# Attention heads of the fourth stage as one stream, their q and k stacked in pairs through DRAM

## The reference

```python
c_kv = h @ w_dkv.T
q = (h @ w_q.T).reshape(B, S, 16, 16)
k = (c_kv @ w_uk.T).reshape(B, S, 16, 16)
v = (c_kv @ w_uv.T).reshape(B, S, 16, 16)
scores = einsum('bqhd,bkhd->bhqk', q, k) * 0.25 + alibi_bias(S)   # -inf above the diagonal
attn = softmax(scores, axis=-1)
out = einsum('bhqk,bkhd->bqhd', attn, v).reshape(B, S, 256) @ w_o.T
x = x + out
```

## Time and profile before

| | us |
|---|---|
| median of 3 runs | 636.63 |
| lowest, highest | 632.98, 636.9 |
| the profiled execution | 632.82 |
| its span, from first to last instruction | 631.0 |
| PE busy, DVE, ACT, POOL | 580.0, 422.4, 250.6, 110.1 |
| mean granted TensorE clock | 0.888 of 2.4 GHz |

### The profile page before, as it was taken

One profiled execution on the slowest core, in us unless ns is written; L12 is line 12 of the kernel. 1 busy time (PEld: TensorE's weight loads), 2 busy tenths in 40 slices (PEclk: granted clock), 3 DMA queues, 4 the chain that ended last, 5 costly groups with the idle time before them and its releaser, 6 DMA issues.

```text
span 631.0 us, 9323 instructions
## 1 busy us (share of the span) xinstructions
PE 580.0 (92%) x3218; PEld 470.9 (75%) x3218; DVE 422.4 (67%) x1249; ACT 250.6 (40%) x525; POOL 110.1 (17%) x163
## 2 busy tenths in 40 slices
PE   1999999999789999999996798899998999989995
PEld 1888888888568888888885687656666666658885
DVE  3677985877863557748777999764542794315986
ACT  3557434642223433335336244323433363333341
POOL 1001000110110000001006428111211032213442
PEclk9999999999789999999999798955558995558999
DMA  5322202000000000000000300000000000000001
GB/s 174 105 96 76 84 28 57 18 2 0 1 1 1 1 1 2 1 0 2 2 0 2 134 21 1 1 1 0 2 2 1 0 2 1 2 0 2 1 34 34
DMA packets 7102, 14.01 MB, mean 22 GB/s; under 512 B 1296, under 2 KB 3600, under 8 KB 6928
## 3 DMA queue, kind: packets, MB, share of 16 engines
q1 hardware_dynamic: 6000, 12.91, 6.3%
q10 hardware_dynamic: 1056, 0.51, 0.3%
HBM read 12.37 MB, written 1.05 MB: 21 GB/s over the span
## 4 chain that ended last, share of the span: by engine, by line
PE 80%; DVE 11%; issue 4%; ACT 2%; POOL 1%; DMA 1%; ACTq 1%; DVEq 0%; POOLq 0%
PE ps L498 19%; PE ps L500 18%; PE ps L499 18%; PE ps L797 4%; PE ps L814 3%; DVE gel L1293 3%; PE ps L774 3%; PE ps L802 2%; PE ps L744 2%; PE ps L786 2%; PE ps L508 2%; PE ps L772 2%; PE ps L745 1%; DVE z L1215 1%; DVE gel L1291 1%
## 5 line engine op out<-in xcount | busy, mean ns | idle before, releaser
L498 PE MATMUL ps<-zh,w0u_h 128*128 128x512 f32 x256 | 102.4, 400 | 2.5 <-issue 2.5
L500 PE MATMUL ps<-zl,w0u_h 128*128 128x512 f32 x256 | 101.8, 397 | 0.0
L499 PE MATMUL ps<-zh,w0u_l 128*128 128x512 f32 x256 | 101.5, 396 | 0.0
L945 ACT ACTIVATE gel<-ps 128x512 f32<-128x512 f32 x64 | 38.2, 597 | 104.1 <-PE ps L500 103.9
L1311 DVE TENSOR_TENSOR act<-gel,ps 128x512 f32<-128x512 f32 x64 | 43.8, 684 | 52.7 <-ACT gel L945 52.7
L498 PE MATMUL ps<-w0d_h,ah 128*128 128x256 f32 x256 | 73.3, 286 | 1.3 <-DVE al L1318 1.0
L1571 DVE CUSTOM_DVE_ANT_0 ps<-ps,bias 128x128 f32<-128x128 f32 (+1 forms) x128 | 43.1, 381 | 44.2 <-PE ps L774 43.9
L499 PE MATMUL ps<-w0d_h,al 128*128 128x256 f32 x256 | 72.4, 283 | 0.0
L500 PE MATMUL ps<-w0d_l,ah 128*128 128x256 f32 x256 | 72.4, 283 | 0.0
L1318 DVE TENSOR_TENSOR al<-act,ah 128x512 fp32r<-128x512 f32 x64 | 43.9, 686 | 23.5 <-ACT ah L951 23.2
L498 PEld LDWEIGHTS ps<-zh,w0u_h 128*128 128x128 f32 x256 | 48.7, 190 | 12.0 <-issue 2.9
(11 more groups left out here) (189 smaller groups left out, 1243.0 us busy)
## 6 DMA issues: line engine op xcount, KB each, us to landing
stage<-in_w_dram SPq DMA_DIRECT2D x16, 384.0 KB, 3.0
stage<-in_w_dram SPq DMA_DIRECT2D x8, 256.0 KB, 2.6
pbt<-in_sel_dram SPq DMA_DIRECT2D x1, 1280.0 KB, 7.3
x<-in_x_dram SPq DMA_DIRECT2D x2, 512.0 KB, 5.3
out_dram<-x SPq DMA_DIRECT2D x2, 512.0 KB, 2.9
va<-in_wa_dram SPq DMA_DIRECT2D x1, 896.0 KB, 5.0
post_b<-in_posts_dram ACTq DMA_DIRECT2D x1, 388.0 KB, 6.1
bias<-in_bias_dram SPq DMA_DIRECT2D x1, 192.0 KB, 7.8
```

The source lines that it names most:

```text
L498: pe.matmul(o, lh, rh, start=start, stop=False, **kw)
L499: pe.matmul(o, ll, rh, start=False, stop=False, **kw)
L500: return pe.matmul(o, lh, rl, start=False, stop=stop, **kw)
L945: nc.scalar.activation(gel[:, n % 2, :], ps[:, 2 * (n % 2), :], ACT.Gelu_apprx_tanh).then_inc(gelu_s, 1)
```

## The change

- q and k (hi and lo parts) of a block are written to an internal DRAM tensor `split_out`, eight DMAs of 128 x 512 per block. The sync queue then reads them back in eight halves of 4 head pairs (half a sequence's heads each), nine DMAs per half, into `q_raw` and `k_raw`, two buffers. A pair is stacked in 96 rows: q of both heads, three groups of 32 rows; k once for each head, with zeros in the other head's rows. The zeros are loaded once, in ffn1.
- POOL copies each pair with rounding to fp32r into rings of 8 slots, `qs` (256 columns) and `ks` (2 x 256): four pairs, then `ln_scale` of the next block, two more pairs, and from then on one pair before every second mask.
- `scores` uses 96 rows. Rows 96 to 127 of `ks` hold constants (position and -1), those of `qs` the transposed minima, which ACT copies straight into the slots; `scores_t` is two matmuls of 128 rows, and L797 goes, with `sel` and `shift_t`. `shift_turn` has four transposes for three.
- The two loops become one of 64 heads and 12 steps. Block 1's transposes, c, q and k stand in steps 5 to 17, its v in steps 27 and 44, each with one PSUM bank; the output rounds follow every 16 heads. The first projections are in the order c, q0, k0, k1, q1, v. ACT copies v to `va` (before: DVE). DVE's statistics for block 1 stand ahead of the loop and its `normalise` in step 2, those for the next stage in steps 57 and 61, and the transposes for it in step 66.
- q's and k's hi and lo parts for block 1 wait for the writes of block 0. `oth` and `otl` now lie in spare parts of `ah`, `al`, `qh` and `ql`.

The diff, cut to its core:

```diff
-ROWS = 3 * HD
-STEP = 64
+PAIRS = HEADS // 2
+PAIR = 2 * HD
+K_ROWS = 3 * PAIR
+ONE_COL = K_ROWS + 4
 GROUP = 4
-ONE_ROW, LATE_ROW = 2 * GROUP, 32
 TURN = 6
 SUM = 12
 OUT_STEPS = (27, 29, 32, 34, 36, 38)
-Z_STEP = 33
-Q_STEPS = (36, 38, 40)
+Z_HALVES = (5, 7)
+C_STEP = 9
+Q_STEPS = (11, 15)
+K_STEPS = (13, 17)
+V_STEPS = (27, 44)
+LN_STEPS = (57, 61)
+Z_STEP = 66
+HALF = PAIRS // 2
+SLOTS = 8
+AHEAD = 6
+STACKED = 16 * 9
...
-        qs = sb("qs", [P, HEADS // 2, BLK], F32R)
-        ks = sb("ks", [P, HEADS // 2, BLK], F32R)
+        qs = sb("qs", [P, SLOTS, SEQ], F32R)
+        ks = sb("ks", [P, SLOTS, 2, SEQ], F32R)
+        q_raw = sb("q_raw", [P, 2, HALF, SEQ])
+        k_raw = sb("k_raw", [P, 2, HALF, 2, SEQ])
...
+            def write(b, m, kind):
+                hi, lo, hi_s, lo_s = ((qh, ql, qh_s, ql_s), (kh, kl, kh_s, kl_s))[kind]
+                sp.wait_ge(hi_s, 2 * b + m + 1)
+                sp.wait_ge(lo_s, 2 * b + m + 1)
+                for i, src in enumerate((hi, lo)):
+                    sp.dma_start(split_out[kind, i, b, P * m:P * (m + 1), :], src[:, m, :].bitcast(F32))\
+                      .then_inc(written_s[kind][m], 16)
+
+            def read(h):
+                n, m, i = h // 2, h % 2, h % 2
+                b, cols, rows = n // 2, slice(n % 2 * SEQ, (n % 2 + 1) * SEQ), slice(P * m, P * (m + 1))
+                if h >= 2:
+                    sp.wait_ge(pair_s, HALF * (h - 1))
+                sp.wait_ge(written_s[0][m], 32 * (b + 1))
+                for part, hl in enumerate((0, 1, 0)):
+                    sp.dma_start(q_raw[PAIR * part:PAIR * (part + 1), i, :, :],
+                                 split_out[0, hl, b, rows, cols].rearrange("(a r) q -> r a q", r=PAIR))\
+                      .then_inc(stack_s[i], 16)
+                sp.wait_ge(written_s[1][m], 32 * (b + 1))
+                for part, hl in enumerate((0, 0, 1)):
+                    src = split_out[1, hl, b, rows, cols].rearrange("(a e r) q -> e r a q", e=2, r=HD)
+                    for e in range(2):
+                        r = PAIR * part + HD * e
+                        sp.dma_start(k_raw[r:r + HD, i, :, e, :], src[e]).then_inc(stack_s[i], 16)
...
+                sp.dma_start(k_raw[0:K_ROWS, :, :, :, :].rearrange("p i a e q -> p (i a e q)"),
+                             zeros_in.partition_broadcast(K_ROWS)).then_inc(zero_s, 16)
+                sp.wait_ge(zero_s, 16)
+                for m, kind in ((0, 0), (0, 1), (1, 1), (1, 0)):
+                    write(0, m, kind)
+                for h in range(4):
+                    read(h)
+                for m, kind in ((0, 0), (0, 1), (1, 0), (1, 1)):
+                    write(1, m, kind)
+                for h in range(4, 8):
+                    read(h)
...
+            def round_pair(gp):
+                h, slot = gp // HALF, gp % SLOTS
+                if gp % HALF == 0:
+                    pool.wait_ge(stack_s[h % 2], STACKED * (h // 2 + 1))
+                if gp >= SLOTS:
+                    pool.wait_ge(t_ps, 2 * (gp - SLOTS) + 2)
+                nc.gpsimd.tensor_copy(qs[0:K_ROWS, slot, :], q_raw[0:K_ROWS, h % 2, gp % HALF, :])
+                nc.gpsimd.tensor_copy(ks[0:K_ROWS, slot, :, :], k_raw[0:K_ROWS, h % 2, gp % HALF, :, :]).then_inc(pair_s, 1)
...
+                    elif b == 0:
+                        for gp in range(HALF):
+                            round_pair(gp)
+                        ln_scale(st.p + 1)
+                        for gp in range(HALF, AHEAD):
+                            round_pair(gp)
+                        for hd in range(4 * HEADS):
+                            if hd % 2 == 0 and hd // 2 + AHEAD < 4 * PAIRS:
+                                round_pair(hd // 2 + AHEAD)
+                            if hd == LN_STEPS[0] - TURN + 1:
+                                ln_scale(st.p + 2)
                             mask(hd)
...
                 split_ready(p)
+                project_c(0)
                 project_q(0, 0)
+                project_k(0, 0)
+                pe.wait_ge(acc_s, E * f0 + U1 * st.d1 - 1)
+                project_k(0, 1)
                 project_q(0, 1)
-                project_c(0)
...
+                project_v(0)
+                project_v(1)
+                for s in range(4 * HEADS + SUM):
+                    if s < 4 * HEADS:
+                        scores(s)
+                    if s % GROUP == 1 and GROUP < s < 4 * HEADS + GROUP:
+                        shift_turn(s // GROUP - 1)
+                    if TURN <= s < 4 * HEADS + TURN:
+                        scores_t(s - TURN)
+                    if s % GROUP == 0 and s >= SUM:
+                        for c in range(2):
+                            pv((s - SUM) // GROUP, c)
+                    for n in range(3):
+                        if s - HEADS * n in OUT_STEPS:
+                            i = OUT_STEPS.index(s - HEADS * n)
+                            (out_back, out_turn, out_project)[i % 3](n, i // 3)
+                    if s in Z_HALVES:
+                        half_transposes(p + 1, Z_HALVES.index(s))
+                    if s == C_STEP:
+                        split_ready(p + 1)
+                        project_c(1)
+                    if s in Q_STEPS:
+                        project_q(1, Q_STEPS.index(s))
+                    if s in K_STEPS:
+                        project_k(1, K_STEPS.index(s))
+                    if s in V_STEPS:
+                        project_v(2 + V_STEPS.index(s))
+                    if s == Z_STEP and st.after:
+                        pe.wait_ge(sm_s, 4 * HEADS)
+                        transposes(p + 2)
...
             def scores(hd):
 
-                t0, h = (hd // HEADS % 2) * SEQ, hd % HEADS
-                r0, r1 = STEP * (h % 2), STEP * (h % 2) + ROWS
+                slot, e = head(hd)
+                if e == 0:
+                    pe.wait_ge(pair_s, hd // 2 + 1)
+                if hd == 0:
+                    pe.wait_ge(qh_s, 2)
+                    pe.wait_ge(ql_s, 2)
                 if hd >= 2:
                     pe.wait_ge(sm_s, hd - 1)
-                pe.matmul(ps[:, score_bank(hd), 0:P], qs[r0:r1, h // 2, t0:t0 + P], ks[r0:r1, h // 2, t0:t0 + P],
+                pe.matmul(ps[:, score_bank(hd), 0:P], qs[0:K_ROWS, slot, 0:P], ks[0:K_ROWS, slot, e, 0:P],
                           start=True, stop=True)
-                pe.matmul(ps[:, score_bank(hd), P:3 * P], qs[r0:r1, h // 2, t0 + P:t0 + 2 * P],
-                          ks[r0:r1, h // 2, t0:t0 + 2 * P], start=True, stop=True).then_inc(s_ps, 1)
+                pe.matmul(ps[:, score_bank(hd), P:3 * P], qs[0:K_ROWS, slot, P:SEQ],
+                          ks[0:K_ROWS, slot, e, :], start=True, stop=True).then_inc(s_ps, 1)
 
             def shift_turn(g):
                 if g == 0:
                     pe.wait_ge(shz_s, 2)
-                if g % 8 == 0:
-                    pe.wait_ge(kl_s, g // 4 + 2)
+                    pe.wait_ge(v_s, 2)
+                    pe.wait_ge(acc_s, E * f0 + U1 * blocks_before_attn1)
                 pe.wait_ge(shl_s, g + 1)
                 if g:
                     pe.wait_ge(sht_s, g)
-                for i, block in enumerate((3, 0, 2)):
-                    mm = pe.transpose(ps[:, 2, i * P:(i + 1) * P], shift[:, g % 2, block, :], ident[:, :])
+                for i in range(4):
+                    mm = pe.transpose(ps[:, 2, i * P:(i + 1) * P], shift[:, g % 2, i, :], ident[:, :])
                 mm.then_inc(sht_ps, 1)
 
             def scores_t(hd):
 
-                t0, h = (hd // HEADS % 2) * SEQ, hd % HEADS
-                r0, r1 = STEP * (h % 2), STEP * (h % 2) + ROWS
+                slot, e = head(hd)
                 bank = turned_bank(hd)
+                if hd == 0:
+                    pe.wait_ge(rows_s, 2)
                 pe.wait_ge(sht_s, hd // GROUP + 1)
                 if hd >= 2:
                     pe.wait_ge(exp_s, hd - 1)
-                pe.matmul(ps[:, bank, 0:3 * P], sel[r0:r0 + LATE_ROW + 1, 4, hd % GROUP, :],
-                          shift_t[r0:r0 + LATE_ROW + 1, hd // GROUP % 2, :], start=True, stop=False,
-                          skip_group_check=True)
-                pe.matmul(ps[:, bank, 0:P], ks[r0:r1, h // 2, t0 + P:t0 + 2 * P], qs[r0:r1, h // 2, t0 + P:t0 + 2 * P],
-                          start=False, stop=False, skip_group_check=True)
-                pe.matmul(ps[:, bank, P:3 * P], ks[r0:r1, h // 2, t0:t0 + P], qs[r0:r1, h // 2, t0:t0 + 2 * P],
-                          start=False, stop=True, skip_group_check=True).then_inc(t_ps, 1)
+                pe.matmul(ps[:, bank, 0:P], ks[:, slot, e, P:SEQ], qs[:, slot, P:SEQ],
+                          start=True, stop=True)
+                pe.matmul(ps[:, bank, P:3 * P], ks[:, slot, e, 0:P], qs[:, slot, :],
+                          start=True, stop=True).then_inc(t_ps, 1)
...
+                prepare(p + 1, 0)
+                for s in range(4 * HEADS + SUM):
```

(45 more changed lines are left out.)

388 lines of the change are left out of this document (148 added, 240 removed).

## The result

The changed kernel takes 587.71 us, median of 4 runs (586.8 to 590.47), beside 634.81 for the kernel before; the ratio is 0.9265 [0.9214, 0.9316]. The profiled execution is 587.15 us with a span of 585.4. The forecast was 585, from 564 to 616.

The account below looks back on a forecast made before the run. PE at half clock was taken to bound the head loops. From first scores at 414, stall 5, groups 70, rest 19.5, slow start 3 and drain 4 end at 515.5, 52 us less than today: 585 us, range 564 to 616.

Parts of the forecast that it names:

- The clock bounds the stage, and width raises it: Head loops: PE bounds them at half its clock; matmuls using 48 or 33 of 128 rows keep it low.
- PE's removed work: Head loops: 64 L797 and 64 stack matmuls go, 47.3 us on the path, leaving 114 us at unchanged clock.
- rival B: Head loops: the clock stays at 1.2 GHz, groups of 5.4, with waits 5.7 us; 617 us, chance 0.18.
- Group of 4.4 us: Head loops: four heads want 4.1 us on PE, 3.5 DVE, 4.1 POOL; with waits 4.4, 16 make 70 us.
- the rest of 19.5: PE's other work in the stream: output rounds, second block's transposes and projections, next stage's transposes, 19.5 us together.
- POOL: Head loops: two rounding copies per pair take 1.23 us (bounds 0.8 and 2.03), with masks 4.1 us a group.
- C: Head loops: weight loads hide and POOL costs its lower bound, groups of 3.4 us; 569 us, chance 0.12.
- D: Head loops: DVE locks POOL out, 4.2 us a pair of copies; 648 us, slower than before, chance 0.04.
- The start: Before the head loops: first scores wait for the DRAM round trip and start at 414, not 409.8; upper bound 420.
- The second stall: Early head loops: bias_min(3) queues behind the next block's normalise, which waits for POOL's ln_scale; 5 us.
- Clock at the start: First heads: 1.2 GHz until the dense projections of steps 9 to 17 raise the clock, 3 us.
- The drain: End of the head loops: draining the last steps takes 4 us.

## Why the prediction was right, step by step

- **The clock bounds the stage, and width raises it: shown.** Narrow scores in the changed kernel cost 42 us; wide ones in the kernel before, once L797 is gone, give 39. The forecast called this the reading of one pair of windows; both kernels now bear it out. That 48 rows in one kind are enough to lose it was not foreseen, and the gaps were given too large a part: the kernel before with wide scores keeps 1.00 behind the same 1.04 us. (Beside the full-width matmuls, 486.6 to 489.8 in the earlier trace rows also holds a pv, at 488.95.)
- **PE's removed work, 47.3 us at an unchanged clock: the step that failed**, though the forecast's own sum did not rest on it. Half the stacks gave -1.1% and not 12 us, since the stacks held the clock. L797 gave 22.5 for 23, but by luck: some 10 us of its own and the rest with the clock. And without the clock's gain the new loop does not take 114 us: with narrow scores it is 146 (414.94 to 561.07, first scores to the end of the last pv, mean clock 0.58 for 0.64). Old matmuls ran two at a time in different rows; subtracting their time counts time that was shared. So **rival B's price was wrong**: B took 1.28 us off a group at half clock for L797, where 0.64 came off; a group takes 7.06 us, 6.4 without the out_back in it, not 5.4; and a kernel whose clock stays low takes 0.9931 of before, some 630, not 617. B's 0.18 should have stood for hardly any gain.
- **Group of 4.4 us and the rest of 19.5.** The shortest group takes 4.07; the forecast had 4.1 for PE alone and 0.3 for waits. Groups and rest together were priced too high: (70 + 19.5)/16 = 5.6 us a group, where the run with the out steps apart takes 72.6 us for 15 groups at 1.00 (pv from 442.50 to 515.14), 4.8. In the changed kernel 15 groups take 83.9 (438.82 to 522.74), 5.6 again, but with the two falls of the clock in them. In the shortest group, on PE's timeline, a 128-column score matmul is 0.06 ahead of the next where no load is exposed and 0.13 where one is, against the 0.17 of the earlier trace rows:
```profile
463.65 0.23 PE L825 MATMUL ps<-ks,qs 96*128 96x128 f32 x1
463.71 0.33 PE L827 MATMUL ps<-ks,qs 96*128 96x256 f32 x1
463.92 0.30 PE L851 MATMUL ps<-qs,ks 128*128 128x128 f32 x1
464.05 0.33 PE L853 MATMUL ps<-qs,ks 128*128 128x256 f32 x1
```
- **POOL.** A pair is 0.90 us, not 1.23: copies of 0.39 (256) and 0.61 us (512). The mask's time per element was too much for them; 0.8 was the nearer end, and POOL was not on the path of the groups, as its doubled copies show. C's condition was met in part, and D fell: the normalise beside POOL's copies took 2.09 us, POOL's copies kept 0.61.
- **The start.** First scores 415.28 for 414, with the queue's order as argued: four stores fewer ahead of the reads made PE's idle time 3.3 us shorter. The second stall is 3.0 us of idle PE (0.36 and 2.67) for 5, since the pairs and the normalise were shorter.
- **Clock at the start and its falls: a term too small, and one put at nothing.** 3 us were counted up to the dense projections. They did raise it, at about 434.8, as named, but that is 19.5 us into the stream and not some 10; PE is busy 14.8 us of these at 0.50, so up to 7.4 by an estimate from these numbers. The falls at 475.7 and 499.8 were not counted: some 14 us at half clock, and the spaced out steps, with no such fall in the loop, are 7 us faster (11 in the stage itself).
- **The drain, another term too small.** The last head's scores end at 511.8. Up to there the stream took 96.5 us from the first scores, where the forecast had 97.5 (5 + 70 + 19.5 + 3). Behind it stand 11.8 us for the 4 of the forecast:
```profile
511.50:523.60 12.10, 8.93 (x95) 6.74 (x94) 4.89 (x19) 6.38 (x17) 3.87 (x9) 1.00 0.01 2
```
PE waits in it for 0.71 and 1.81 us at out_project; part of its work the forecast had under the rest. These 7.8 us, less the 1.0, and the start 1.3 later make the 8.1 us by which the last pv was late; 1.8 came back behind it.
- **DVE.** The 43.9 us of waiting for scores went to 25.6 (L827 for L774), not "mostly gone".

That the time came within 3 us is in part luck. The forecast was 52 us less; measured are 47.1 between the medians and 45.6 between the spans. Of the profiled execution the forecast said 581, and it took 587.15, 6 us more. 585 was counted from a median 3.8 us above the profiled execution of the kernel before; with more runs that median is 634.81, and the changed kernel's lies only 0.6 above its profiled execution. And the 6 us are themselves a balance: groups, rest and second stall priced too high, against a longer drain, a longer low start and the falls of the clock. The mechanism, the clock, was right.

## What to carry to other kernels

When PE is busy and its clock is at the lower level, first ask how many rows its matmuls use: as the runs of this kernel show, folding parts into one wide operand can be worth more than the matmuls it removes, and removing wide matmuls can cost time. Before subtracting a matmul's time, look in the timeline whether it runs beside another, and after a run check the clock before believing that the time saved was its own. And a microsecond won anywhere in such a stage may not come through if waits behind it let the clock fall; here spacing those out came first, and mending the start paid only then.

## What the runs showed of the hardware that was not expected

- 48-row matmuls in one of the two score kinds, PE busy 20.00 of 20 us, kept the granted clock at 0.50 (632.38 us); 96 and 128 rows gave 1.00 with PE busy 33.75 of 40. Half of the 96 rows of k are zeros there, and the clock is at 1.00 all the same. Where between 48 and 96 rows the change lies was not tried.
- Matmuls over rows 0 to 48 and 64 to 112 started within 0.01 us of each other. Over 112 shared rows the group went from 6.44 to 9.45 us at half clock.
- POOL's fp32 to fp32r copies of 96 x 512 took 0.61 us, less than half of the two-input subtraction of the earlier trace rows.
- Two waits of 0.95 and 1.12 us, 3.4 us apart, were followed by 10 us at 0.51 though PE was busy in all of them (500 to 510); two of 1.42 us, 7 apart, were not.
